# Down products of two feed-forwards turned round: stationary weights, three float32r passes, the sum by channel

## What is computed

```python
x = x + tanh(g_xattn[0]) * wkv(layernorm(x), ctx)                # a scan over tokens, per channel
x = x + tanh(g_ffn[0])   * peer_ffn(layernorm(x))                # the feed-forward that is changed
x = x + tanh(g_xattn[1]) * linear_attention(layernorm(x), ctx)
x = x + tanh(g_ffn[1])   * mixture_of_experts(layernorm(x))      # 8 experts, 2 per token, and a shared one
...
# peer_ffn of one token row x (256 channels)
mlp = silu(x @ gate_w) * (x @ up_w) @ down_w                     # 1024 hidden channels
ew  = silu(einsum(x, down_embed[indices])) * softmax(scores)     # 8 of 512 experts, picked by routing
out = mlp + einsum(ew, up_embed[indices])
```

## Time and profile before

| | us |
|---|---|
| median of 3 runs | 522.52 (520.04 to 523.59) |
| span of the profiled execution, first to last instruction | 517.5 |
| TensorE busy in that span | 449.8 (87%) |
| VectorE / ScalarE / GpSimd busy | 360.9 / 246.7 / 154.5 |
| mean granted TensorE clock, share of full | 0.967 |

### The profile page before, as it was taken

How to read it: one execution, slowest core, us unless ns; L and a number is a source line. 1 busy time by engine, 2 the same in 40 slices (tenths; PEclk the granted TensorE clock), 3 DMA queues, 4 the chain that set the end, 5 groups by cost and what they waited for, 6 DMA issues and landing times. The chain is left out here.

```text
span 517.5 us, 7233 instructions
## 1 busy us (share of the span) xinstructions
PE 449.8 (87%) x2142; PEld 355.1 (69%) x2142; DVE 360.9 (70%) x1034; ACT 246.7 (48%) x452; POOL 154.5 (30%) x156
## 2 busy tenths in 40 slices
PE   1617999599999889999999999898999799899991
PEld 1315688368578666878778886787777588788851
DVE  6896779995289986565987966978867554531173
ACT  3618574363576346346125315470453454955540
POOL 3955342330002131110000001032336014477771
PEclk9966999799999989999999999999999999999997
DMA  8500312000300000960000000123232423346394
GB/s 303 187 31 30 103 31 83 0 1 0 101 2 0 2 0 14 310 178 0 1 1 1 1 0 2 32 71 102 90 115 83 123 73 91 114 139 208 85 385 153
DMA packets 32965, 42.00 MB, mean 81 GB/s; under 512 B 3483, under 2 KB 26781, under 8 KB 32928
## 3 DMA queue, kind: packets, MB, share of 16 engines
q1 hardware_dynamic: 28224, 32.28, 20.7%
q0 software_dynamic: 3744, 8.42, 4.4%
q10 hardware_dynamic: 960, 0.86, 0.5%
HBM read 24.97 MB, written 18.39 MB: 84 GB/s over the span
## 5 line engine op out<-in xcount | busy, mean ns | idle before, releaser
L660 PE MATMUL acc<-w_down,act_s 128*128 128x256 f32 x384 | 92.2, 387 | 0.9 <-DVE act_s L1386 0.9
L660 PEld LDWEIGHTS acc<-w_down,act_s 128*128 128x128 f32 x384 | 74.6, 195 | 13.2 <-DVE act_s L1386 1.3
L636 PE MATMUL ring<-xt_h,up_l 128*128 128x512 f32 x160 | 70.5, 441 | 2.9 <-DVE xt_l L1356 1.5
L1601 POOL TENSOR_TENSOR rstd<-var_eps,minus_half 128x4 f32<-128x4 f32 x14 | 14.9, 1068 | 176.5 <-DVE var_eps L1186 176.5
L637 PE MATMUL ring<-xt_l,up_h 128*128 128x512 f32 x160 | 63.8, 399 | 0.0
L638 PE MATMUL ring<-xt_h,up_h 128*128 128x512 f32 x160 | 63.7, 398 | 0.0
L1098 ACT ACTIVATE act_s<-ring 128x512 f32<-128x512 f32 x48 | 28.6, 597 | 59.9 <-PE ring L638 59.6
L631 PE MATMUL ring<-small,xn 128*128 128x128 f32 x160 | 23.6, 297 | 26.2 <-ACT xn L998 14.1
L699 PE MATMUL ring<-up_e,act_s 128*128 x184 | 44.3, 383 | 2.3 <-issue 2.0
L1637 POOL DMA_INDIRECT x_rows<-main_a,slots x32 | 31.1, 971 | 43.7 <-ACT main_a L1119 34.8
L1390 DVE TENSOR_TENSOR act_s<-ring,act_s 128x512 f32<-128x512 f32 x32 | 22.0, 686 | 30.8 <-PE ring L638 21.0
(11 more groups left out here) (275 smaller groups left out, 987.8 us busy)
## 6 DMA issues: line engine op xcount, KB each, us to landing
main_b<-x_rows SPq DMA_DIRECT2D x22, 257.0 KB, 2.8
x_rows<-v_t SPq DMA_DIRECT2D x1, 3983.5 KB, 16.7
up_l<-y_rows SPq DMA_DIRECT2D x5, 512.0 KB, 7.0
stage<-in_w_mlp SPq DMA_DIRECT2D x8, 256.0 KB, 2.6
up_e<-in_w_moe SPq DMA_DIRECT2D x8, 256.0 KB, 2.6
x_rows<-v_t SPq DMA_DIRECT2D x1, 1927.5 KB, 22.8
x_nat<-in_x SPq DMA_DIRECT2D x7, 256.0 KB, 7.7
out_x<-x_nat SPq DMA_DIRECT2D x6, 256.0 KB, 5.2
```

The costliest lines, as they stand in the source:

```text
L636: pe.matmul(out, wl, xh, start=first, stop=False, skip_group_check=True)
L660: last = pe.matmul(acc[t // 2][:, t % 2, :], act_s[n % RING][:, tok], w_down[:, u, :], start=u == 0 and t % 2 == 0, stop=final, skip_group ...
```

## The change

The downs of mains 2 and 3 are turned round. Stationary is now the weight block, 128 hidden x 128 output channels, moving are the activations, 128 hidden x 512 tokens; the product runs in three float32r passes, and `acc` holds output channels on the partitions. That needs high and low halves of both operands:

- `dsplit` (main 2 only, one in each of its steps 1 to 12): ScalarE copies `w_down` of the unit to a float32r tile (128 x 256), GpSimd subtracts it from `w_down` in place. The first waits for `route 2`'s product Q.
- `hid_copy` (mains 2 and 3, every unit): ScalarE copies `act_s` to `hid_h` (128 x 512) one step after that unit's Silu (unit u: Silu in step u+1, copy in step u+2); GpSimd subtracts it from `act_s` in place, in the same step. `hid_h[0]` and `hid_h[1]` lie on `v_t`, so the first one of main 2 (step `mlp 2 2`) waits for `rows_cleared`.
- `mlp_out` in two parts: ScalarE copies gate x `acc` to `host_s` (two of 128 x 512) and frees `acc`; TensorE transposes it back (eight 128 x 128) into two ring banks; VectorE adds these to `x_nat`.

The memory for the new tiles is taken from buffers whose use is over. Cut to its core:

```diff
+BY_CHANNEL = (2, 3)
...
-        13: "attn 1 9 10, mlp_in 3 2, moe_in 1 0, mlp 2 14 15, moe_in 1 1",
+        13: "attn 1 9 10, mlp_in 3 2, moe_in 1 0, mlp 2 14 15, mlp_out 2 0, moe_in 1 1",
...
-        1: "mlp_out 2 0, attn_in 2 0, moe_in 1 2, route 3 4",
+        1: "mlp_out 2 1, attn_in 2 0, moe_in 1 2, route 3 4",
...
-LAST = """mlp_out 3 0, attn_in 3 0, shared 0 0 1, shared 1 0, shared 2 0, attn_in 3 1, shared 1 1, shared 2 1,
+LAST = """mlp_out 3 0, shared 0 0, mlp_out 3 1, attn_in 3 0, shared 0 1, shared 1 0, shared 2 0, attn_in 3 1, shared 1 1, shared 2 1,
...
+        if f == BY_CHANNEL[0] and 1 <= part <= MLP_UNITS:
+            SCHED.append(("dsplit", 0, part - 1))
...
 (TensorE, down)
+                if f in BY_CHANNEL:
+                    pe.wait_ge(down_low, u + 1)
+                    pe.wait_ge(hid_low, split_turn(f, u) + 1)
+                    high = down_high_of(u)
+                    for c in range(C):
+                        m = slice(c * P, (c + 1) * P)
+                        last = three_pass(acc[c][:, :, :].rearrange("p t d -> p (t d)"), high[:, m], down_l[:, u, m],
+                                          hid_h[n % RING][:, :], hid_l[n % RING][:, :], u == 0, final)
+                    last.then_inc(down_done, 1)
+                    return
...
+                elif kind == "mlp_out" and part == 1:
+                    pe.wait_ge(acc_copied, C * (BY_CHANNEL.index(g) + 1))
+                    for p in range(2):
...
+                                last = pe.transpose(bank[:, (t * C + c) * P:(t * C + c + 1) * P], host_s[:, c, tok], ident)
...
 (ScalarE)
+            def hid_copy(f, u):
+
+                n = unit_of(f, u)
+                hidden_made(act, n)
+                act.activation(hid_h[n % RING][:, :], act_s[n % RING][:, :], ACT.Copy).then_inc(hid_high, 1)
...
+                    if g in BY_CHANNEL and 1 <= u <= MLP_UNITS:
+                        if g == BY_CHANNEL[0] and u == 1:
+                            act.wait_ge(rows_cleared, 32)
+                            full(act, (("kv", NG - 1), "V", GT - 1))
+                        hid_copy(g, u - 1)
+                elif kind == "dsplit":
+                    u = part
+                    act.wait_ge(down_done, unit_of(BY_CHANNEL[0] - 1, u) + 1)
+                    if u == 0:
+                        full(act, (("route", 2), "Q"))
+                    act.activation(down_high_of(u), w_down[:, u, :], ACT.Copy).then_inc(down_high, 1)
+                elif kind == "mlp_out" and g in BY_CHANNEL and part == 0:
+                    act.wait_ge(down_done, (g + 1) * MLP_UNITS)
+                    act.wait_ge(hid_ready, HID_TURN[("mlp", g, MLP_UNITS - 1)])
+                    for c in range(C):
+                        act.activation(host_s[:, c, :], acc[c][:, :, :].rearrange("p t d -> p (t d)"), ACT.Copy,
+                                       scale=gates[:, 1:2]).then_inc(acc_copied, 1)
...
 (VectorE)
+                elif kind == "mlp_out" and g in BY_CHANNEL:
+                    for p in range(2 if part else 0):
...
+                        free((step, "Y", p), dve.tensor_tensor(out, bank[:, :], out, ALU.add))
...
 (GpSimd)
+                elif kind == "dsplit":
+                    pool.wait_ge(down_high, part + 1)
+                    pool.tensor_tensor(down_l[:, part, :], w_down[:, part, :], down_high_of(part).bitcast(F32),
+                                       ALU.subtract).then_inc(down_low, 1)
+                elif kind == "mlp" and g in BY_CHANNEL and 2 <= part <= MLP_UNITS + 1:
+                    n = unit_of(g, part - 2)
+                    pool.wait_ge(hid_high, split_turn(g, part - 2) + 1)
+                    pool.tensor_tensor(hid_l[n % RING][:, :], act_s[n % RING][:, :], hid_h[n % RING][:, :].bitcast(F32),
+                                       ALU.subtract).then_inc(hid_low, 1)
```

More of the change, by code:

```diff
@@ L91 @@
 UPS = IC * UP + EC * PEER_UP
+BY_CHANNEL = (2, 3)
+MAIN_B_UNITS = IC
+V_ODD_UNITS = EC // C
 def block_cols(w):
@@ L331, in build @@
         minus_mean = sb("minus_mean", [P, 2, GT])
-        v_t = [sb(f"v_t{c}", [P, GN]) for c in range(C)]
-        v_odd = [sb(f"v_odd{c}", [P, GN]) for c in range(C)]
+        v_t, v_odd, hid_h, down_h_odd = [], [], [], []
+        for c in range(C):
+            with nc.sbuf_tensor(f"hid_h{c}", [P, GN], F32R) as words:
+                hid_h.append(words)
+            v_t.append(sb(f"v_t{c}", [P, GN]))
+        for c in range(C):
+            with nc.sbuf_tensor(f"down_h_odd{c}", [P, V_ODD_UNITS * D], F32R) as words:
+                down_h_odd.append(words)
+            v_odd.append(sb(f"v_odd{c}", [P, GN]))
         main_a = [sb(f"main_a{c}", [P, 2, GT * PAD]) for c in range(C)]
+        with nc.sbuf_tensor("down_h_main", [P, MAIN_B_UNITS * D], F32R) as down_h_main:
+            pass
         main_b_words = sb("main_b", [P, C * 2 * GT * PAD])
@@ L350, in build @@
         onehot = sb("onehot", [P, 2, NK, TOPK], BF16)
+        with nc.sbuf_tensor("hid_h2", [P, GN], F32R) as words:
+            hid_h.append(words)
         k_e = [sb(f"k_e{k}", [P, D]) for k in range(2)]
+        with nc.sbuf_tensor("hid_h3", [P, GN], F32R) as words:
+            hid_h.append(words)
         k_r = [sb(f"k_r{k}", [P, D]) for k in range(2)]
@@ L359, in build @@
         xt_f = xt_f_pad[:, 0:C * GN].rearrange("p (c n) -> p c n", c=C)
-        act_s = [sb(f"act_s{k}", [P, GN]) for k in range(RING)]
+        act_s, hid_l = [], []
+        for k in range(RING):
+            with nc.sbuf_tensor(f"hid_l{k}", [P, GN], F32R) as words:
+                hid_l.append(words)
+            act_s.append(sb(f"act_s{k}", [P, GN]))
         host_s = sb("host_s", [P, 2, GN])
@@ L402, in build @@
         up_e = sb("up_e", [P, UPS])
+        with nc.sbuf_tensor("down_l", [P, MLP_UNITS, D], F32R) as down_l:
+            pass
         w_down = sb("w_down", [P, MLP_UNITS, D])
@@ L486, in build @@
         qf_ready = sem("qf_ready")
+        down_high = sem("down_high")
+        down_low = sem("down_low")
+        hid_high = sem("hid_high")
+        hid_low = sem("hid_low")
+        acc_copied = sem("acc_copied")
         wsplit_h = sem("wsplit_h")
@@ L561, in hidden_made, with down_high_of, split_turn @@
                 freed(eng, ((kind, f), "B", u))
+        def down_high_of(u):
+            if u < MAIN_B_UNITS:
+                return down_h_main[:, u * D:(u + 1) * D]
+            c, k = divmod(u - MAIN_B_UNITS, V_ODD_UNITS)
+            return down_h_odd[c][:, k * D:(k + 1) * D]
+        def split_turn(f, u):
+            return BY_CHANNEL.index(f) * MLP_UNITS + u
         def sent(eng, grp):
@@ L655, in down @@
                     pe.wait_ge(acc_free, 2 * f)
+                final = u == MLP_UNITS - 1
+                if f in BY_CHANNEL:
+                    pe.wait_ge(down_low, u + 1)
+                    pe.wait_ge(hid_low, split_turn(f, u) + 1)
+                    high = down_high_of(u)
+                    for c in range(C):
+                        m = slice(c * P, (c + 1) * P)
[3 more added lines that the diff above has]
+                    return
                 hidden_made(pe, n)
-                final = u == MLP_UNITS - 1
                 for t in range(GT):
@@ L926, in _ @@
                     close_bank(key, last)
+                elif kind == "mlp_out" and part == 1:
+                    pe.wait_ge(acc_copied, C * (BY_CHANNEL.index(g) + 1))
+                    for p in range(2):
+                        key = (step, "Y", p)
+                        bank = open_bank(key)
+                        for t in range(2):
+                            tok = slice((2 * p + t) * P, (2 * p + t + 1) * P)
+                            for c in range(C):
+                                last = pe.transpose(bank[:, (t * C + c) * P:(t * C + c + 1) * P], host_s[:, c, tok], ident)
+                        close_bank(key, last)
                 elif kind == "shared" and part == 0:
@@ L1103, in _ @@
                             act.activation(host_s[:, 0, :], bank[:, :], ACT.Copy).then_inc(free_sem((step, "EY")), 1)
+                    if g in BY_CHANNEL and 1 <= u <= MLP_UNITS:
[12 more added lines that the diff above has]
+                    act.wait_ge(hid_ready, HID_TURN[("mlp", g, MLP_UNITS - 1)])
+                    for c in range(C):
+                        act.activation(host_s[:, c, :], acc[c][:, :, :].rearrange("p t d -> p (t d)"), ACT.Copy,
+                                       scale=gates[:, 1:2]).then_inc(acc_copied, 1)
+                    act.wait_ge(acc_copied, C * (BY_CHANNEL.index(g) + 1))
+                    act.sem_inc(acc_free, C)
                 elif kind == "moe":
@@ L1396, in _ @@
                         free((step, "S", p), residual(x_nat[:, b:b + 2, :].rearrange("p t d -> p (t d)"), bank[:, :], 3))
+                elif kind == "mlp_out" and g in BY_CHANNEL:
+                    for p in range(2 if part else 0):
+                        b = main_seqs(g)[2 * p]
```

(3 more changed lines are left out.)

## The result

The change makes the kernel slower: 539.50 us (539.16 to 541.52, six runs) against 521.97 (520.04 to 523.76, six runs), a ratio of 1.0341 with a 95% interval of 1.0309 to 1.0372. I had forecast 529.2, with 534 as the upper end: the sign was right, the size was not.

The account below looks back on a forecast made before the run. TensorE bounds most stretches, VectorE keeps pace in two, a chain through VectorE bounds main 3's end. +0.4 up to there and tail +6.3 give +6.7 us on a 517.5 span: 524.2, median 529.2; range 521.5 to 534.

Parts of the forecast that it names:

- GpSimd and VectorE together: Up to the end of main 3: new GpSimd subtractions slow VectorE in one or two hits, +1.0 us; bounds 0 and 8.1.
- the third leg: From the Silu of unit 2 of main 2 to `slots` of main 2's rows: forecast -2.2 us.
- Rival C: Subtractions hold up VectorE eleven times 0.74 us where it paces (244 to 268, 321.6 to 356.6): 536.3 us; chance 0.12.
- Start of main 2: First `hid_copy` waits on ScalarE for the clearing DMAs, making attention of main 0 late: +2.6 us, bounds 0 and 4.0.
- the prediction's own mark: Attention of main 0, its exponentials at 240.83 before, begins 2.7 us late.
- Rest of main 2 and main 3: Shorter downs save 2.3 us in main 2's units 5 to 11, 1.3 in main 3's units 4 to 7; transposes +0.4.
- The low half behind the scatters: End of main 3: the last low half follows six scatters on GpSimd, so the last down starts 4.3 us later.
- The way back and the slow clock: From the last down's start to the end, +2.0 us: last down at 1.2 GHz, longer way of the sum, 1.9 given back.
- A: TensorE bounds to the end of main 3, slack absorbs the late attention, twenty units save 0.33: 523.1 us; chance 0.27.
- B: End of main 3: the six scatters start earlier and don't hold up the last low half: 517.4 us; chance 0.06.
- From span to median: Whole kernel: the median of the runs lies 5.0 us above the profiled span, so 524.2 became 529.2 us.

Follow-up runs that it names:

- experiment 1: The changed kernel with GpSimd's 36 subtractions replaced by writes of zeros into the same low halves: 527.90 us.
- 2: The kernel before with 36 subtractions on dead buffers, which nobody waits for, added to GpSimd's queue: 530.45 us.
- experiment 3: The changed kernel with the clearing DMAs reading the other value buffer, so the first copy to the hidden block's high half doesn't wait for them: 536.05 us.
- experiment 5: The changed kernel with zeros for the 36 subtractions, clearing DMAs on the other buffer and tile 10's scatters behind the last low half: 522.81 us.
- 4: The changed kernel with the two scatters of token tile 10 moved behind the last hidden block's low half in GpSimd's queue: 537.31 us.
- 6: The changed kernel with clearing DMAs on the other buffer, tile 10's scatters behind the last low half, shared expert's products ahead of the last down: 533.84 us.
- 9: The changed kernel with clearing DMAs on the other buffer and tile 10's scatters behind the last low half, shared products left in place: 533.33 us.

## Why the prediction was wrong, point by point

- **GpSimd and VectorE together: the step that failed.** It stood at +1.0 us, with 8.1 as its upper bound; it measured some 10 (1: 11.6 less; 2: 9.5 more; the third leg: 8.4 with it, -1.5 without in experiment 1). Rival C named the mechanism and 536.3 us, and I gave it 0.12; that its 8.1 came so near was in part luck, since it counted eleven hits in two stretches where there were six. The reasoning behind the low value was a misreading of the earlier trace rows: "three of that line's four executions were not slowed". GpSimd runs nothing beside those three, at 146.74, 234.11 and 293.06 in the timeline of before. Its next instructions there, with the idle time ahead of each:

```profile
153.24 1.11 POOL L1601 TENSOR_TENSOR rstd<-var_eps,minus_half 128x4 f32<-128x4 f32 x1 [38.52 <-DVE var_eps L1186]
...
257.44 1.01 POOL L1601 TENSOR_TENSOR rstd<-var_eps,minus_half 128x4 f32<-128x4 f32 x1 [32.69 <-DVE var_eps L1186]
...
310.75 1.01 POOL L1601 TENSOR_TENSOR rstd<-var_eps,minus_half 128x4 f32<-128x4 f32 x1 [36.77 <-DVE var_eps L1186]
```

The row was not one in four but one in one. And the upper bound counted hits in the two stretches alone. Set beside the same instruction of before, 13 VectorE instructions of the changed kernel that run beside a subtraction lost over 0.3 us each, 10.3 us together: six of them, 4.0 us, in those two stretches, four, 2.6 us, in the rest of main 2, and three, 3.7 us, at the end of main 3, a chain of small VectorE instructions. Two of the last lost 1.67 and 0.98 us (DVE and POOL of the changed kernel):

```profile
393.73 1.84 DVE L1538 CAST s_if<-s_idx 128x8 f32<-128x8 uint32 x1
...
394.26 1.27 POOL L1724 TENSOR_TENSOR hid_l<-act_s,hid_h 128x512 fp32r<-128x512 f32 x1
...
400.23 1.35 POOL L1724 TENSOR_TENSOR hid_l<-act_s,hid_h 128x512 fp32r<-128x512 f32 x1 [4.70 <-ACT hid_h L1032]
...
400.46 1.25 DVE L1596 TENSOR_TENSOR kv_sum<-chosen,kv_sum 128x64 f32<-128x64 f32 x1
```

As the third leg changes by 9.9 us, nearly all of this reached the path, also where the prediction had TensorE set it.

- **Start of main 2: +2.6, measured 4.4** in that trace, 3.4 by experiment 3. The mechanism was right. The size was off because I let VectorE's routing take up part of it, and because the clearing DMA landed after 25.4 us here; over the traces with the change's buffer it lands after 22.4 to 25.4 us, so the wait is not the same in every execution. By the prediction's own mark, attention's step at 240.83, it was 5.1 us (245.97, 0.4 of them from ahead of it), above the upper bound of 4.0.
- **Rest of main 2 and main 3: -2.3, +0.4 and -1.3.** Each down saves its 0.33 (1.39 us measured), but without subtractions and without the wait the leg gives 0.9 us, not 3.2 (experiment 5). 0.8 of the difference is the copies, told under 5; for the rest, less of the saving stays than I had kept, and which unit gives how much I didn't separate.
- **The low half behind the scatters: 4.3, measured 4.0,** of which 2.0 is the wait for the scatters (4 takes it away).
- **The way back and the slow clock: 2.0 in all, measured 2.8.** Here the parts came out too. The transposes of attention came 8.3 us later behind `slots` than before (423.95 for 402.41, less the 13.2), where the forecast had 8.2, and 1.5 of these were given back by the end (21.5 late there, 20.0 at the end), where it had 1.9. The clock did fall to 1.2 GHz (the last down took 2.70 us, 411.20 to 413.90), and a new wait of 2.17 us for a ring bank, which I had not counted, came with it. Experiments 6 and 9 bear on the 2.4 of the slow clock: with the last down at 2.4 GHz, and two products fewer in TensorE's way, the transposes came 1.9 us sooner behind it; no run separates the two.
- **Rivals A and B.** Their premises fell: nothing absorbed the wait, and the last low half did stand behind the scatters.
- **From span to median.** The 5.0 us between them was too much for a constant: after's profiled execution took 539.28, 1.8 above its span. Before's profiled execution was one of its quicker ones, so by spans the change costs 20.0 and by medians 17.5.

## What to carry to other kernels

Work moved to GpSimd is not free because GpSimd is idle: where it reads SBUF, price each instruction against what VectorE has to do at that time, and take the price whole: here nearly all of it reached the end, also outside the stretches where VectorE paced before. Before taking "it was slowed once in four" from a row, look at what the other engine did beside each of the four. And when an edit saves on an engine at 87%, ask first for each stretch who would have to be late for the saving to count: here 7.9 us of shorter products left 0.9 us of gain, net, ahead of `slots` (experiment 5).

## What the runs showed of the hardware

- A VectorE instruction that reads SBUF twice waited for the end of GpSimd's subtraction beside it (0.22 us became 1.33), one with a PSUM input didn't (0.69 stayed 0.69), and GpSimd's writes of zeros, 0.53 us for 128 x 512, held up next to nothing.
- Cutting the subtraction into four pieces shortened the hold of `L1541` and made more of them: the whole was nearly the same (369.2 for 371.7 busy), while GpSimd's own time for a hidden block rose from 1.28 to 1.8 us (43.7 us for 96 pieces).
- A VectorE conversion of 128 x 8 with a single SBUF input took 1.84 us for 0.17 as well, and so was the norm's `xn` held, one block of 128 x 256 and two scalars a token: four of them took 2.18 us, the first beside a subtraction (330.48), for 1.39 before.
